# Moved chain products, ScalarE's upper halves, 58 side columns, and layer 1 added by accumulating DMAs

## The reference

```python
xh = conv1x1(gn(x), w_in, b_in)                        # 256 channels
pooled = mean(xh, axis=(2, 3))
hcx = relu(pooled @ kg_w1.T + kg_b1)
kernels = (hcx @ kg_w2.T + kg_b2)                      # 3 x 3 per image and channel
y = depthwise_conv3x3(xh, kernels)
x = x + conv1x1(y * tanh(softplus(y)), w_out, b_out)   # layer 0
x = x + relu(real(ifft(mix(fft(gn(x)) * mask))))       # layer 1, linear up to the relu
```

## Time and profile before

| | us |
|---|---|
| median of 3 runs | 3799.29 (3797.97 to 3801.11) |
| the profiled execution: its time | 3798.16 |
| the profiled execution: its span | 3796.4 |
| TensorE busy | 3658.1 (96% of the span) |
| VectorE busy | 3522.8 (93%) |
| ScalarE busy | 3316.2 (87%) |
| GpSimd busy | 2774.9 (73%) |
| transfers on SP's queue | 397.66 MB, 30.1% of 16 engines' span |
| transfers on GpSimd's queue | 67.13 MB, 12.2% |

### The profile page before, as it was taken

How to read it: one execution, slowest core, us unless ns; L and a number is a source line. 1 busy time by engine, 2 the same in 40 slices (tenths; PEclk the granted TensorE clock), 3 DMA queues, 4 the chain that set the end, 5 groups by cost and what they waited for, 6 DMA issues and landing times. The chain is left out here.

```text
span 3796.4 us, 65618 instructions
## 1 busy us (share of the span) xinstructions
PE 3658.1 (96%) x21868; PEld 2251.8 (59%) x21868; DVE 3522.8 (93%) x4778; ACT 3316.2 (87%) x5860; POOL 2774.9 (73%) x2388
## 2 busy tenths in 40 slices
PE   4899999999999999999999999999999999999997
PEld 2455666656566666666656666565666656666664
DVE  5999999999999999999999999999999999999996
ACT  3888989899898998989999898998989989897775
POOL 3566777877778777777777777777777777777773
PEclk8999999999999999999999999999999999999999
DMA  4323444444444444444444444444444444443333
GB/s 152 78 70 104 130 128 132 125 130 131 122 139 119 137 127 127 136 122 132 126 128 132 128 130 125 131 133 123 134 128 129 130 125 134 125 131 95 92 94 126
DMA packets 148159, 468.99 MB, mean 124 GB/s; under 512 B 17328, under 2 KB 18416, under 8 KB 147568
## 3 DMA queue, kind: packets, MB, share of 16 engines
q1 hardware_dynamic: 110960, 397.66, 30.1%
q0 software_dynamic: 36864, 67.13, 12.2%
HBM read 397.61 MB, written 134.22 MB: 140 GB/s over the span
## 5 line engine op out<-in xcount | busy, mean ns | idle before, releaser
L654 PE MATMUL psA<-hi,wa 128*128 128x288 f16 (+4 forms) x9792 | 1852.2, 280 | 0.8 <-DVE wtmp L876 0.8
L907 DVE SCALAR_TENSOR_TENSOR accB<-xh,vectors,accB 128x1024 f32<-128x1024 f32 x1280 | 1640.4, 1282 | 0.0
L1118 POOL TENSOR_TENSOR tsum<-tsum,tprod 128x1024 f32<-128x1024 f32 x512 | 1210.5, 2364 | 293.9 <-ACT tprod L407 271.2
L919 DVE SCALAR_TENSOR_TENSOR accS<-side,vectors,accS 128x448 f32<-128x448 f32 x2048 | 1399.1, 683 | 19.2 <-ACT accS L416 10.0
L654 PE MATMUL psA<-lo,wa 128*128 128x288 f16 (+5 forms) x4896 | 1320.6, 279 | 0.0
L654 PEld LDWEIGHTS psA<-hi,wa 128*128 128x128 f16 x9792 | 931.0, 98 | 336.6 <-issue 66.9
L696 PE MATMUL psBO<-wm,woutt 128*128 128x512 f32 x2048 | 966.4, 594 | 12.5 <-DVE X L929 11.8
L1122 POOL TENSOR_TENSOR X<-X,zt 128x512 f32<-128x512 f32 x480 | 610.9, 1273 | 363.3 <-DVE accB L907 289.5
L696 PEld LDWEIGHTS psBO<-wm,woutt 128*128 128x128 f32 x2048 | 385.4, 190 | 497.5 <-issue 496.6
L1110 POOL TENSOR_TENSOR lo<-X,hi 128x1024 f16<-128x1024 f32 x256 | 546.9, 2136 | 182.6 <-DMA hi<-in_x_dram 111.4
L407 ACT ACTIVATE tprod<-xh,vectors 128x1024 f32<-128x1024 f32 x512 | 583.2, 1139 | 32.6 <-POOL tsum L1118 32.5
(11 more groups left out here) (166 smaller groups left out, 3363.4 us busy)
## 6 DMA issues: line engine op xcount, KB each, us to landing
X<-in_x_dram SPq DMA_DIRECT2D x256, 512.0 KB, 3.3
out_dram<-X SPq DMA_DIRECT2D x256, 512.0 KB, 2.6
XS<-in_x_dram SPq DMA_DIRECT2D x240, 512.0 KB, 3.3
hi<-in_x_dram POOLq DMA_DIRECT2D x256, 256.0 KB, 4.3
X<-in_w_t_dram SPq DMA_DIRECT2D x2, 1152.0 KB, 18.3
w1t<-in_w_t_dram SPq DMA_DIRECT2D x1, 256.0 KB, 2.7
wint<-in_w_in_t_dram SPq DMA_DIRECT2D x1, 128.0 KB, 2.3
woutt<-in_w_out_t_dram SPq DMA_DIRECT2D x1, 128.0 KB, 2.6
```

Of the source, the lines that this page charges most:

```text
L654: last = mm(o[:, r:r + q, 0:cols], w, src[:, at:at + q, SIDE + dx - 1:SIDE + dx - 1 + cols], start=(tap == ORDER[0] and w is wh and src is ...
L907: V.scalar_tensor_tensor(out=rows_of(accB[:]), in0=xh[:, 8 * j + dy:8 * j + dy + 8, dx:dx + W], scalar=kk[i % 2][:, TAPS + k:TAPS + k + 1] ...
L919: V.scalar_tensor_tensor(out=side_out(), in0=side[:, 8 * j + dy:8 * j + dy + 8, dx:dx + SIDE], scalar=kk[i % 2][:, k:k + 1], in1=side_out( ...
L1118: P.tensor_tensor(tsum[:], tsum[:], tprod[:], ALU.add).then_inc(s_ta, 1)
```

## The change

Six edits:

1. SIDE goes from 56 to 58: two more columns of set A go to VectorE, and CW, the convolution's width, from 72 to 70.
2. `small_0(n)` stands behind the whole of `conv(n, 0)` (in the first slot of an image behind six taps).
3. The upper halves of the tap matrices and of the wide weights are cast on ScalarE (`taps_high`, `weights_high`); GpSimd keeps the lower halves. ScalarE's other small copies move by a place or two in its list.
4. Layer 1 is no longer added in SBUF. SP stores the strip after layer 0, three slots behind instead of twenty, and GpSimd issues one accumulating DMA for each half, which adds `zt` to what stands in the output in memory. The next load into a strip's place waits for the store and for layer 1's product, and `relu` for the accumulate that last read its half of `zt`.
5. At the start w2 is loaded behind strips 0 and 1; ScalarE casts it first, and VectorE's two subtractions stand among the statistics, before those of strips 8 and 10. ScalarE's three `taps_high` come before it empties the first two strips.
6. Four GpSimd multiplications by a column take another instruction.

```diff
-SIDE = 56
+SIDE = 58
@@ SP: load_x
                     eng.wait_ge(s_out[m % 4], 16 * (m // 4 + 1))
+                    eng.wait_ge(s_lm, 2 * m + 2)
@@ SP: store, and the order
-                eng.wait_ge(s_add, 2 * m + 2)
+                eng.wait_ge(s_x1, 2 * m + 2)
...
-            for k in range(2):
-                eng.dma_start(w2t[:, k], w2_t[:, k]).then_inc(s_w2in[k], 16)
+                    for k in range(2):
+                        eng.dma_start(w2t[:, k], w2_t[:, k]).then_inc(s_w2in[k], 16)
...
-                if n >= LAG1 + 1:
-                    store(n - LAG1 - 1)
+                if 3 <= n < N - STRIPS + 3:
+                    store(n - 3)
@@ ScalarE
+            def taps_high(i, u):
+                eng.wait_ge(s_wt, 3 * i + u + 1)
+                act(wa[:, i % 2, 0, 3 * u * C:3 * (u + 1) * C], wtmp[:], ACT.Copy).then_inc(s_wsh, 1)
+
+            def weights_high(i):
+                eng.wait_ge(s_wn, i + 1)
+                act(wb[:, i % 2, 0, :], wn[:], ACT.Copy).then_inc(s_wbh, 1)
@@ relu
-                    eng.wait_ge(s_add, 2 * m + t - 1)
+                    eng.wait_ge(s_acc[t], 16 * m)
@@ ScalarE, the start
-            stats_group("x", 0, small_bank(0))
-            pooled_out(0, small_bank(0))
-            hidden_out(0, small_bank(0))
             for k in range(2):
                 eng.wait_ge(s_w2in[k], 16)
                 act(w2p[:, 0, k], w2t[:, k], ACT.Copy).then_inc(s_w2h, 1)
+            stats_group("x", 0, small_bank(0))
+            pooled_out(0, small_bank(0))
+            weights_high(0)
+            hidden_out(0, small_bank(0))
             kernels_out(0, small_bank(0))
             bias_out(0, small_bank(0))
+            for u in range(3):
+                taps_high(0, u)
@@ ScalarE, slot
                     tap_product(n + 1, 0)
+                if s == 0 and b >= 1:
+                    taps_high(b, 2)
+                if n + 1 < N:
+                    tap_product(n + 1, 1)
                 if s == 12 and build:
+                    weights_high(b + 1)
                     pooled_out(b + 1, small_bank(1))
                 if s == 3 and b >= 1:
                     layer1_bias(b - 1, small_bank(1))
-                if n + 1 < N:
-                    tap_product(n + 1, 1)
+                if s in (14, 15) and build:
+                    taps_high(b + 1, s - 14)
+                mish_conv(n, 0)
                 if s == 13 and build:
                     kernels_out(b + 1, small_bank(1))
-                mish_conv(n, 0)
@@ TensorE, slot
-                conv(n, 0, slice(0, 5))
+                first = n % STRIPS == 0
+                conv(n, 0, slice(0, 6 if first else TAPS))
                 small_0(n)
-                first = n % STRIPS == 0
-                conv(n, 0, slice(5, 6 if first else TAPS))
@@ VectorE, the start
             for c in range(2 * STRIPS):
+                if c in (16, 20):
+                    k = (c - 16) // 4
+                    eng.wait_ge(s_w2h, k + 1)
+                    V.tensor_tensor(w2p[:, 1, k], w2t[:, k], w2p[:, 0, k], ALU.subtract).then_inc(s_w2l, 1)
@@ GpSimd
-                P.tensor_copy(wa[:, i % 2, 0, part], wtmp[:]).then_inc(s_wsh, 1)
-                eng.wait_ge(s_wsh, k)
+                eng.wait_ge(s_wsh, 3 * i + u + 1)
                 P.tensor_tensor(wa[:, i % 2, 1, part], wtmp[:], wa[:, i % 2, 0, part], ALU.subtract).then_inc(s_wsl, 1)
...
             def add(m, t):
+                b, at = m // STRIPS, m % STRIPS * SP + t * TP
                 eng.wait_ge(s_re, 2 * m + t + 1)
-                P.tensor_tensor(half(m, t), half(m, t), zt[:, t, :], ALU.add).then_inc(s_add, 1)
+                eng.wait_ge(s_out[m % 4], 16 * (m // 4 + 1))
+                eng.dma_start(out[b, :, at:at + TP], zt[:, t, :], accum_op=ALU.add).then_inc(s_acc[t], 16)
```

More of the change, by code:

```diff
@@ L159, in conv_preact_kernel @@
         s_re = sem("s_re")
-        s_add = sem("s_add")
+        s_acc = [sem(f"s_acc{t}") for t in range(2)]
         s_b0 = sem("s_b0")
@@ L294, in _ @@
                         load_stat(c + 1)
-            for m in range(N - LAG1 - 1, N - STRIPS):
-                store(m)
             for s in range(STRIPS):
@@ L305, in _ @@
             eng.wait_ge(s_sin, 16 * STATS)
+            for t in range(2):
+                eng.wait_ge(s_acc[t], 16 * (N - STRIPS))
         @block.scalar
@@ L946, in _ @@
             V.tensor_scalar(valid[:], valid[:], -1.0, None, ALU.add).then_inc(s_valid, 1)
-            for k in range(2):
-                eng.wait_ge(s_w2h, k + 1)
-                V.tensor_tensor(w2p[:, 1, k], w2t[:, k], w2p[:, 0, k], ALU.subtract).then_inc(s_w2l, 1)
             for u in range(3):
@@ L1046, in fold @@
                     eng.wait_ge(s_wbl, i)
-                P.tensor_scalar(wn[:], wint[:], st["x"]["r"][:, 0:1], None, ALU.mult).then_inc(s_wn, 1)
+                P.tensor_tensor(wn[:], wint[:], st["x"]["r"].broadcast_to([C, HID]), ALU.mult).then_inc(s_wn, 1)
             def pool_bias(i):
@@ L1067, in kernel_bias @@
                 eng.wait_ge(s_pl, i + 1)
-                P.tensor_scalar(bk[:], k2[:, 0:TAPS], bp[i % 2][:, 0:1], None, ALU.mult).then_inc(s_bst, 1)
+                P.tensor_tensor(bk[:], k2[:, 0:TAPS], bp[i % 2][:, 0:1].broadcast_to([C, TAPS]), ALU.mult).then_inc(s_bst, 1)
                 eng.wait_ge(s_bst, 2 * i + 1)
@@ L1073, in kernel_bias, with taps_low, weights_low @@
                 P.tensor_tensor(bx[:, 32:32 + TAPS], bk[:], bh[:], ALU.subtract).then_inc(s_bxr, 1)
-            def taps_halves(i, u):
-                k, part = 3 * i + u + 1, slice(3 * u * C, 3 * (u + 1) * C)
-                eng.wait_ge(s_wt, k)
-                P.tensor_copy(wa[:, i % 2, 0, part], wtmp[:]).then_inc(s_wsh, 1)
-                eng.wait_ge(s_wsh, k)
+            def taps_low(i, u):
+                part = slice(3 * u * C, 3 * (u + 1) * C)
+                eng.wait_ge(s_wsh, 3 * i + u + 1)
                 P.tensor_tensor(wa[:, i % 2, 1, part], wtmp[:], wa[:, i % 2, 0, part], ALU.subtract).then_inc(s_wsl, 1)
-            def weights_halves(i):
-                eng.wait_ge(s_wn, i + 1)
-                P.tensor_copy(wb[:, i % 2, 0, :], wn[:]).then_inc(s_wbh, 1)
+            def weights_low(i):
                 eng.wait_ge(s_wbh, i + 1)
@@ L1088, in fold_1 @@
             def fold_1(i):
-                P.tensor_scalar(lpt[:, i % 2, :], lt[:], st["1"]["r"][:, 0:1], None, ALU.mult).then_inc(s_lpt, 1)
+                P.tensor_tensor(lpt[:, i % 2, :], lt[:], st["1"]["r"].broadcast_to([C, C]), ALU.mult).then_inc(s_lpt, 1)
             def high(n):
@@ L1134, in _ @@
             pool_bias(0)
-            weights_halves(0)
+            weights_low(0)
             hidden_low(0)
@@ L1138, in _ @@
             for u in range(3):
-                taps_halves(0, u)
+                taps_low(0, u)
             for k in range(1, EXTRA + 1):
@@ L1150, in slot @@
                 if s == 0 and b >= 1:
-                    taps_halves(b, 2)
+                    taps_low(b, 2)
                 if m >= 1:
@@ L1163, in slot @@
                 if s in (14, 15) and build:
-                    taps_halves(b + 1, s - 14)
+                    taps_low(b + 1, s - 14)
                 if m >= 0:
@@ L1177, in slot @@
                 if s == 12 and build:
-                    weights_halves(b + 1)
+                    weights_low(b + 1)
                 if s == 1 and b >= 1:
```

## The result

| | median us | ratio to before, 95% interval |
|---|---|---|
| before | 3799.43 | 1 |
| after | 4373.88 (4357.20 to 4381.23) | 1.1503 (1.1481 to 1.1526) |

Forecast 3760, range 3740 to 3820: wrong in sign. The profiled execution took 4374.05 (span 4372.2). What came true is the first rival, the landing of `hi`.

A forecast was written before the change was run, and what follows sets the result against it. TensorE was taken as the bound, VectorE near. Images 1 to 14 -49.3 us, image 15 -2.6, image 0 -0.6, start +12.5, end +2: together -38, from 3798.16 to a forecast of 3760, range 3740 to 3820.

The forecast's parts named there:

- the first rival: Transfers delay `hi`: costs from a landing of 6.5 us, at 7.0 gives 3878; chance 0.22 for well past the cover.
- the cover of `hi`: Each slot: `hi` may land 6.5 us after issue before TensorE's wide product waits for `lo`; so cost 0.
- Landing 5.0 to 5.7: Casting load of `hi` beside two 512 KB transfers of SP, each costing 0.7 us, 1.4 together.
- The prediction's price at 7.0: If `hi` landed 7.0 us after its issue, 0.5 us lost in each of 236 slots, 118 in all.
- Take turns packet by packet: Transfer engines alternate between queues, so SP's full queue at most doubles `hi`'s byte-moving part; landing never gets near 6.5.
- The accumulates' own landing: Layer 1's accumulating DMAs in GpSimd's queue: 3.5 us taken, 5.9 from above; out of `hi`'s way at 3.5.
- Side columns: 56 to 58 side columns: TensorE loses 0.165 us a slot (13.76 to 13.60), 2.63 an image.
- Small products: Moved behind the ninth tap, they end TensorE's waits for the mean and pooled products: -1.89 us an image.
- Slot 0: ScalarE's upper-half cast makes `lo` late; TensorE waits 1.5 us, two waits of 0.34 fall in: +1.0 an image.
- The start: w2 loaded earlier and upper casts first on ScalarE: +10.3 and +2.2, together +12.5 us on the path.
- The end: Relus of strips 238 and 239 wait for the accumulates of the strip before: +2 us (0 to +6).
- The other rivals: VectorE bounds plain slots at 13.70: 3784, 0.20 shared with landing just past cover; waits return at bank's release: 3788, 0.05.

The follow-up runs named there:

- e4: Changed kernel with no DMA of layer 1 (one element copied instead; output lacks layer 1 except in the last image), SP's order as changed: 4084.74 us, one run.
- e2: Changed kernel with the load of `hi` issued behind the first sum of taps instead of the second: 3793.07 us, ratio 0.9978 to before.
- e8: e2 with the start in its old order and both halves cast on GpSimd again: 3754.77 us, ratio 0.9877 to before.
- e3: Changed kernel with plain DMAs for the accumulating ones (layer 1 overwrites the output), SP's order as changed: 4138.15 us, one run.
- e7: Kernel before with only the small products moved behind the ninth tap and ScalarE's copies in their new places: 3800.22 us, ratio 0.9999.
- e12: e8 with the small products back behind the fifth tap: 3752.38 us, ratio 0.9870 to before.
- e9: e2 with the old start only, the halves still on ScalarE: 3785.44 us, ratio 0.9957 to before.
- e1: Changed kernel with layer 1 added in SBUF on GpSimd again and SP's stores and loads in old order: 3818.16 us, ratio 1.0045 to before.
- e6: Kernel before with SIDE = 58 alone: 3777.39 us, ratio 0.9935.

## Why the prediction was wrong

- **The step that failed** is the cover of `hi`, with the landing that was set against it. "Landing 5.0 to 5.7" is 8.4 (7.0 with no accumulate at all), and "`hi` may land 6.5 after its issue" is 5.46. The cover was read at one edge, where TensorE asks for `lo`; but if `lo` comes that late, the next `hi` is issued late too, since its issue stands behind this `lo` and two sums in GpSimd's list, and the second sum waits for a product that ScalarE can't write before the first is done. The loop of 8.14 us plus the landing has to fit into the slot. The prediction's price at 7.0, 0.5 a slot, was 267 / 236 = 1.13 in e4. In the trace of before the loop could be read from `lo` at 1809.43 (rows 8) to the issue behind it:

```profile
1818.76 0.58 POOL L1100 DMA_DIRECT2D hi<-in_x_dram  x1
```

That is 9.33; the loop first uses up this slack, down to 8.14.
- **The landing itself** was summed transfer by transfer, 0.7 each. The place was read rightly, "all beside `hi`": the statistics load is issued 1.33 us ahead of `hi`, the store 0.95 ahead, the next strip's load 1.19 behind it (medians of the same 78 slots), where before the last two came 4.11 and 6.73 behind. The size was not: two more loads of 512 KB take the landing from 4.3 to 7.0 (e4), 2.7 and not 1.4. The price of one transfer, 0.7, was carried over to a burst whose times had not been worked out.
- **"Take turns packet by packet"** was used to argue against this. The Trainium skill (DMA: Bandwidth & Descriptors, Queues, rings and completion order) says that an engine turns after a packet. The reading "at most double the part of `hi` that moves bytes, landing never gets near 6.5" did not hold: in e4 `hi` is alone in GpSimd's queue and lands in 7.0, twice the whole of the quickest landing of before, 3.5. The trace of before spoke against it too, in a stretch that rows 9 leave out. At the start, beside SP's loads of the first strips, its three first loads of `hi` took 8.3 to 12.1 us, the first of them 8.3 (issued at 12.35, `lo` at 20.68):

```profile
L1100 POOL DMA_DIRECT2D hi<-in_x_dram x3: 550/554/737, 12.3 to 13.6; - x3
...
DMA to landing us min/median/max: 8.3/10.1/12.1
```

Unequal packets don't explain it plainly. The queue rows give 1.8 KB a packet to GpSimd's queue and 3.6 to SP's, but for `hi` that counts what is written: the 397.61 MB read from memory fit only if each `hi` reads its 512 KB of float32 (256 x 0.524 MB for X, 240 for XS, 256 for `hi`: 394.3 MB), so its packets read 3.6 KB too. Why the landing grows as it does stays open.
- **The accumulates' own landing**, 3.5 taken, is 4.1 (4.9 in e2 and e8), and their issue 0.86 us where 0.58 to 1.27 was allowed. Beside a casting load their reading and adding costs 236 of the 575 us (e3), a plain write of the same bytes 53.
- **Side columns**: -0.17 a plain slot against -0.165; -23 in all against some -39. The mechanism was right for the plain slots; slot 0 is at VectorE's pace and loses 0.13, slot 2 gains nothing and slot 4 loses 0.15, slots 13 and 14 gain half, and image 0 was 3 us longer, in one execution each, where about none was forecast.
- **Small products**: -28 forecast, -0.4 measured. That the waits end was right; that time ends with them was not, in e7 and in e12. TensorE's idle time was counted as time of the image in slots whose pace it does not set. What does was not isolated; after e12 the chain over GpSimd and ScalarE is a reading.
- **Slot 0**: +1.0 forecast, +1.66 (e9 to e8). TensorE's wait of 1.5 is 1.71 and was read rightly; of the two waits set against it, 0.38 each in e8, one fell in and one stayed, at 0.47, and slot 1 lost 0.32, which the forecast did not have.
- **The start**: +12.5 forecast, +13.9 (e1), 12.1 between e2 and e8. VectorE's statistics ended at 47.5, forecast 47.2. The parts were less well divided: 7.7 forecast for w2's order and 4.8 for the upper halves, 6.0 and 6.1 measured.
- **The end**: +2 forecast for the accumulates. From the first tap of the last image to the end it is 280.0 us, 278.5 before, but 280.5 in e1, which has none; the term is not shown.
- **The other rivals**: plain slots of 13.56 to 13.59 in e1 rule out VectorE as the bound. In e7 no wait for the bank's release stands in TensorE's list; what came in place of the removed waits was `lo`.

The small terms together: -23.2 (e6) - 0.4 (e7) + 13.9 (start) + 15 x 1.66 (slot 0) = +15.2, and e1 measured +16.5.

## What to carry to other kernels

Before a transfer is called covered, follow what must be finished before its next issue: if the consumer of this landing is in that chain, a period can't be shorter than chain + landing, and the cover is the wanted period less the chain. Put the times of all issues of one period on a line: at a mean share of 0.61 the transfer engines stood idle 5 us and were then full, and moving one issue ahead of two others in its list was worth 581 us. An idle wait of the busiest engine counts only in slots whose pace it sets, and a cast handed to an engine that works in order costs its place in the list (here `lo` 2.79 us later) and not its 0.5 us.

## What was unexpected in the hardware

An accumulating DMA of 256 KB in memory took GpSimd 0.86 us to issue, against 0.56 for a plain one (e3), and landed in 4.1 against 2.6:

```profile
L1138 POOL DMA_DIRECT2D out_dram<-zt x480: 539/561/617, 379.7 to 4091.0; - x160
...
DMA to landing us min/median/max: 2.3/2.6/8.3
```

With the same 192.99 MB, GpSimd's queue had 105984 packets and a share of 29.3% of the transfer engines in the changed kernel, and 75264 packets and 17.6% in e3.
